# A two-layer vision kernel on one core: quotient of the recurrence by logarithm and Newton step, gated products of the second attention split, bias rows moved

## The chip, the cores and the metric

The kernel runs on one core of one Trainium2 chip. The metric is the device time of one execution in microseconds. The kernel before was run three times: median 424.29 us, lowest 422.48, highest 426.02.

## What is computed

64 images (3 x 64 x 64) become 1024 tokens of 192 channels; then come four blocks on these, each added to its input. The reference, cut to what matters here:

```
h = tok(x)                                   # shifted patches, layernorm, product with W
h = h + attention0(layernorm(h))             # 12 heads, 16 tokens per image
h = h + experts(layernorm(h))                # 8 experts, top 2, gates; y = gelu(x w1 + b1) w2 + b2
h = h + rwkv(layernorm(h))                   # below
h = h + attention1(layernorm(h))             # qkv has a gated low-rank part, below

# rwkv: forward and backward scans over the 16 tokens of an image, then
y  = (ef * af + eb * ab + ec * vt) / (ef * bf + eb * bb + ec)
x  = x + sigmoid(h @ Wr_a.T) * y @ Wo_a.T
x  = x + sigmoid(h @ Wr_f.T) * (square(relu(h @ Wk_f.T)) @ Wv_f.T)

# attention1
combine = top-2 gates of softmax(x @ Wg.T + bg)          # 8 experts
hw    = (x @ A + ba) * combine                           # rank 16 of each expert: 128 rows
qkv   = x @ Wqkv.T + bqkv + 2 * (hw @ Bm + combine @ bb)
out   = softmax(q k^T / 4) v @ Wproj.T + bproj
```

## The kernel before

The program is written out by hand for the five engines; each runs its own list in order and waits on semaphores. Tokens lie in eight tiles of 128; `hf` is a half of four tiles, `pr` a pair of tiles. The accumulator memory (PSUM) has eight banks, and `plan_fills` (a count over the whole program) gives each result a bank in turn; TensorE waits in `free` until the reader of the bank's last content has gone. To keep precision with f16 products, every operand is split into a high part (ScalarE rounds it to f16) and a low part (VectorE subtracts). So for nearly every step there is a chain: TensorE fills a bank, ScalarE copies the high part, VectorE subtracts the low part, TensorE multiplies both. `busy(name, n)` issues n products on TensorE (`early_a`, 128x512) that nobody reads.

*Experts.* Step u of 16 makes two chunks of 128 hidden units: TensorE multiplies (`h`), ScalarE applies Gelu twice (L871, L876), VectorE subtracts (L1406), and in the step after TensorE makes `y`, which VectorE adds to H with the gate (L1420). The rows `b2x`, `sel` and the clear of `ct3` (L1383 to L1391) are made by VectorE ahead of step 0, and ScalarE waits for them (`sel_ready`) before it copies the transposed gates behind step 3. In step 3 VectorE reads the logits of the second router (L1295), whose bank is one that the next chunks want.

*Recurrence.* 192 channels x 1024 tokens are three blocks of 128x512. `RECURRENCE_ORDER` sets the order of VectorE: `maxima`, `states` (four scans, L1473 and L1475), `sums` (two products, L1514 and L1515) and `outputs`. GpSimd makes one product per block for `states` (`weighted`) and three for the sums (`denominator`). TensorE adds three f32 terms each into `num` and `den`. `outputs` then is, on VectorE,

```
V.scalar_tensor_tensor(start(Af, b), start(rT, b), 1.0, bank(("num", b)), ALU.add, ALU.mult)   # L1521
V.reciprocal(start(E2b, b), bank(("den", b)))                                                  # L1526
V.tensor_tensor(start(E1b, b), start(Af, b), start(E2b, b), ALU.mult)                          # L1528
V.tensor_tensor(sy_lo[b], start(E1b, b), sy_hi[b], ALU.subtract)                               # L1530
```

with ScalarE's copy `sy_hi` (L931) between the last two. The output products `wo` follow, then a layernorm and the feed-forward part (`ffn_low`, `ffn_out`).

*Second attention.* VectorE does `ffn_out(1)`, clears `cstack` (L1582), does `x_low`, `gates_by_rank(0)` (router and ranks, copied to `crep1`, L1589) and `gated(0)`: TensorE transposes `crep1` (bank `ce`) and makes `la = x A`; ScalarE copies `ce` three times (L977 to L979); VectorE subtracts (L1596) and makes `hwF = (la + ba) * ce` (L1603); ScalarE rounds it (L982); VectorE subtracts (L1606). Then it makes the statistics and normalizations of tiles 4 to 7. TensorE's `qkv(hf)` fills five slots (QA, KA, VA, KVB, QB), in each five products of x and four of the gated part, the gated ones between the fourth and fifth of x; all wait for the low part of `hw`. ScalarE rounds each slot (L799), VectorE takes the low part (L1152) and `spread` writes K and V into masked copies for each head (L1162, eight heads in slots 1 and 2, four in slot 3). `ATTENTION_ORDER` is the same for both attentions: in it the second set of value transposes (`values1`) stands ahead of `qkv` of the second half. `gated(1)` stands ahead of `values1`. In VectorE's list it is called by `probabilities` between `softmax_in` (L1175 to L1178) and the second `values` (L1193).

## Time and profile before

| what | us |
|---|---|
| time of the profiled execution | 423.5 |
| its span, first to last instruction | 421.7 |
| TensorE busy | 373.2 (88%) |
| VectorE busy | 353.7 (84%) |
| ScalarE busy | 216.4 (51%) |
| GpSimd busy | 115.6 (27%) |
| mean granted clock of TensorE | 0.954 of full |
| median of three runs | 424.29 |

1.8 us of the execution lie around its span. Lines such as L1526 are lines of the kernel above. In the rows PE is TensorE, DVE VectorE, ACT ScalarE, POOL GpSimd. R, Q, T are large on-chip arrays that most tiles share, PS is PSUM, so that a row's place in time says more of it than its names. A duration in a row is from start to end of one instruction (or of the first to the last of `xN`); instructions of one engine overlap by some 0.1 us.

### The profile page before, as it was taken

To read this page: it belongs to the slowest core of one execution; us is meant where nothing else is said; L and a number is where in the kernel's file an instruction comes from. 1 tells how busy PE (TensorE), PEld (TensorE's weight loads), DVE (VectorE), ACT (ScalarE), POOL (GpSimd) and SP (SyncE) were. 2 spreads that over 40 slices of the span, in tenths; PEclk is the share of its full clock that TensorE was granted. 3 is DMA by queue.
4 is the path that set the end of the run, shared out by engine and by line. 5 is a ranking of instruction groups with operands and counts; after the bars stand their busy time and mean duration, and the time that the engine had idled before them with its cause. 6 is when DMAs were issued, how large, how long until landed. Compare 5 with 4: busy or idle time off the path is not lost.

```text
span 421.7 us, 8868 instructions
## 1 busy us (share of the span) xinstructions
PE 373.2 (88%) x3571; PEld 256.5 (61%) x3571; DVE 353.7 (84%) x787; ACT 216.4 (51%) x364; POOL 115.6 (27%) x151
## 2 busy tenths in 40 slices
PE   2999999797998999999779998887999787797997
PEld 2999958486665675676634443343597336645864
DVE  2979598998879799888989999988998689867872
ACT  2696286656656686796327662011871132454261
POOL 2745307212544481344231286103001010000000
PEclk9999998999598999999999999999999998699996
DMA  7856000400440000000000000000000000000101
GB/s 254 334 150 265 1 2 2 170 3 2 177 193 2 1 2 2 0 2 2 0 2 0 2 0 0 0 2 0 2 2 2 0 2 2 2 0 2 40 3 37
DMA packets 4233, 17.50 MB, mean 42 GB/s; under 512 B 857, under 2 KB 1762, under 8 KB 3682
## 3 DMA queue, kind: packets, MB, share of 16 engines
q1 hardware_dynamic: 4194, 16.95, 10.9%
q8 instruction: 28, 0.46, 0.4%
q14 instruction: 11, 0.09, 0.1%
HBM read 16.16 MB, written 0.79 MB: 40 GB/s over the span
## 4 chain that ended last, share of the span: by engine, by line
DVE 47%; PE 36%; issue 7%; ACT 5%; POOL 2%; DMA 1%; SPq 0%; DVEq 0%; POOLq 0%; ACTq 0%
PE PS L1631 31%; DVE R L1162 5%; DVE R L1475 3%; DVE R L1473 3%; DVE Q L1152 2%; PE PS L1783 2%; DVE H L1420 2%; DVE R L1048 2%; DVE R L1526 2%; POOL rstd L576 2%; DMA T<-tok_w 1%; DVE Q L1406 1%; ACT Q L956 1%; DVE Q L1178 1%; DVE smx L1177 1%
## 5 line engine op out<-in xcount | busy, mean ns | idle before, releaser
L573 POOL TENSOR_SCALAR ve<-mv 128x2 f32<-128x2 f32 (+1 forms) x36 | 10.5, 292 | 125.7 <-DVE mv L1068 102.9
L1631 PE MATMUL PS<-X_hi,R 128*128 128x512 f16 x144 | 39.9, 381 | 0.7 <-DVE gat L1295 0.4
L1631 PE MATMUL PS<-m,Q 128*128 128x192 f16 x384 | 35.4, 251 | 3.2 <-DVE Q L1406 1.9
L1631 PEld LDWEIGHTS PS<-m,Q 128*128 128x128 f16 x384 | 32.5, 100 | 7.1 <-issue 3.1
L1631 PE MATMUL PS<-Q,R 64*64 64x32 f16 (+11 forms) x1024 | 30.6, 193 | 6.9 <-DVE Q L1215 4.4
L1631 PEld LDWEIGHTS PS<-Q,R 64*64 64x64 f16 (+1 forms) x1024 | 29.5, 110 | 9.1 <-issue 6.0
L1631 PE MATMUL PS<-early_a 128*128 128x512 f16 x149 | 35.0, 386 | 0.0
L1631 PE MATMUL PS<-R,K 128*128 128x512 f32 x66 | 31.7, 598 | 3.4 <-DVE R L1515 3.4
L1162 DVE TENSOR_SCALAR R<-Q,K 128x1024 f16<-128x1024 f16 x80 | 32.6, 479 | 0.3
L1631 PE MATMUL PS<-X_hi,late_a 128*128 128x512 f16 (+1 forms) x72 | 26.1, 382 | 6.7 <-DVE X_hi L1142 4.2
L1420 DVE SCALAR_TENSOR_TENSOR H<-PS,gat,H 128x192 f32<-128x192 f32 x64 | 23.0, 410 | 7.2 <-PE PS L1631 6.9
L576 POOL TENSOR_TENSOR rstd<-ve,mhalf 128x2 f32<-128x2 f32 (+1 forms) x36 | 24.8, 690 | 3.0
L871 ACT ACTIVATE Q<-PS,col 128x512 f32<-128x512 f32 x32 | 22.2, 693 | 6.5 <-DVE Q L1406 6.3
L781 ACT ACTIVATE R<-PS 128x1024 f16<-128x1024 f16 x16 | 15.7, 1017 | 17.8 <-PE PS L1783 17.8
L1631 PEld LDWEIGHTS PS<-X_hi,R 128*128 128x128 f16 x144 | 14.2, 99 | 16.8 <-issue 0.8
L1631 PEld LDWEIGHTS PS<-early_a 128*128 128x128 f16 x149 | 14.2, 99 | 15.9 <-issue 0.7
L1631 PEld LDWEIGHTS PS<-R,K 128*128 128x128 f32 x66 | 12.2, 189 | 18.8 <-issue 12.7
L1406 DVE TENSOR_TENSOR Q<-Q 128x512 f16<-128x512 f32 x32 | 22.8, 750 | 0.4 <-ACT Q L876 0.2
L1783 PE MATMUL PS<-id,R 128*128 128x128 f16 x256 | 18.7, 240 | 4.6 <-DVE Q L1204 2.5
L876 ACT ACTIVATE Q<-PS,col 128x512 f16<-128x512 f32 x32 | 22.3, 697 | 0.0
L1631 PE MATMUL PS<-R 128*128 128x192 f32 x128 | 22.2, 328 | 0.1
L1631 PE MATMUL PS<-X_hi,late_b 128*128 128x512 f16 (+1 forms) x72 | 22.0, 379 | 0.0
(246 smaller groups left out, 928.9 us busy)
## 6 DMA issues: line engine op xcount, KB each, us to landing
R<-tok_x SPq DMA_DIRECT2D x8, 480.0 KB, 3.9
T<-tok_w SPq DMA_DIRECT2D x6, 480.0 KB, 7.1
R<-late SPq DMA_DIRECT2D x1, 2632.0 KB, 9.0
T<-moe SPq DMA_DIRECT2D x1, 2304.0 KB, 8.5
T<-moe SPq DMA_DIRECT2D x1, 1728.0 KB, 7.4
R<-full SPq DMA_DIRECT2D x1, 1152.0 KB, 12.3
R<-early SPq DMA_DIRECT2D x1, 776.0 KB, 10.3
out<-H SPq DMA_DIRECT2D x4, 192.0 KB, 1.9
```

What stands on the lines that cost most here:

```text
L573: nc.gpsimd.tensor_scalar(ve[:, t:t + w], mv[:, t:t + w, 1], EPS, None, ALU.add).then_inc(pool_step, 1)
L576: nc.gpsimd.tensor_tensor(rstd[:, t:t + w], ve[:, t:t + w], mhalf[:, 0:w], ALU.pow).then_inc(rstd_ready, 1)
L781: nc.scalar.activation(VA[:, hl, 8 * g:8 * g + 8, :], bank(name).bitcast(F16).rearrange("p (s n) -> p s n", s=8), ACT.Copy).then_inc(v_act ...
L871: nc.scalar.activation(ge[n % 3], bank(("h", n)), ACT.Gelu, bias=b, scale=1.0 / WS).then_inc(act_step, 1)
L876: nc.scalar.activation(hgh[slot], bank(("h", n)), ACT.Gelu, bias=b, scale=1.0 / WS).then_inc(gelu_ready, 1)
L1162: ins = V.tensor_scalar(v[:, :, :, h], w, K[:, mask + h:mask + h + 1], None, ALU.mult)
L1406: V.tensor_tensor(hgl[slot], ge[n % 3], hgh[slot], ALU.subtract).then_inc(hp_ready, 1)
L1420: ins = V.scalar_tensor_tensor(H[:, t], bank(name)[:, C * j:C * j + C], gat[:, 5, t, e:e + 1], H[:, t], ALU.mult, ALU.add)
L1473: link(V.tensor_tensor_scan(dst[:, 0:HALF][:, ::-1], d0, d1[:, ::-1], 0.0, op0, op1))
L1475: link(V.tensor_tensor_scan(dst[:, 1:BW], d0, d1, 0.0, op0, op1))
L1631: return T_.matmul(o, w, x, start=start, stop=stop, skip_group_check=True)
L1783: last = T_.transpose(o[:, P * s:P * s + P], VAbd[:, hl, 8 * g + s], id16[:])
```

## The change

Three parts.

1. *Bias rows.* The three clearings go to GpSimd, ahead of its clearing of `rW0`, and the five small operations become `bias_rows`, called in step 2 of the experts. The clearing of `cstack` goes to GpSimd too, behind the first `wo`.
2. *Quotient.* The product with `r` of block 0 and its Tanh come ahead, beside k and v of block 0 (nine unread products instead of 14). TensorE makes the sums in the order of `QUOTIENT_SUMS`. ScalarE takes Ln of `den` and Exp of the negative; VectorE refines with one Newton step and multiplies (`quotient`); `outputs` is gone. The low parts are steps of their own, the third one behind the first `wo_out`. `sums(1)` stands ahead of `states(2)`. The sign of the Tanh's argument is turned, and with it the sign of both factors.
3. *Gated products.* `adapted(hf)` makes the five products of x for the first two (second half: three) slots with no wait for the gates, then with a wait for the high half (`hw_high_ready`) their three products with it, then with a wait for the low half the rest. The second output pair of `ffn_out(1)` and the statistics of tiles 4 to 7 stand between `gates_by_rank(0)` and `gated(0)` on VectorE. In the second half `gated(1)` comes ahead of `qkv`, and `values1` comes behind `pt`. The unread products of `qkv` (8 and 13) are gone, eight of the 20 before the router too; eight come behind the second router.

```
+                    ("sums", 1), ("states", 2), ("sums", 2), ("quotient", 0), ("quotient", 1), ("low", 0), ("low", 1),
+                    ("quotient", 2))
+QUOTIENT_SUMS = (("num", 0), ("den", 0), ("num", 1), ("den", 1), ("den", 2), ("num", 2))
+SY_HIGH = {0: 1, 1: 2, 2: 5}
+SY_LOW = {0: 4, 2: 6}
+KVR_ORDER = (("k", 0), ("v", 0), ("r", 0), ("k", 1), ("k", 2), ("v", 1), ("v", 2), ("r", 1), ("r", 2))
...
             def decay_steps():
 
                 pool.wait_ge(psum_filled, f.done["pj", 0, 1, 1])
+                nc.gpsimd.memset(b2x[:], 0.0)
+                nc.gpsimd.memset(sel[:], 0.0)
+                nc.gpsimd.memset(ct3[:], 0.0).then_inc(rows_clear, 1)
                 nc.gpsimd.memset(rW0[:], 0.0).then_inc(pool_step, 1)
...
+            weighted(0)
+            weighted(1)
+            denominator(0)
+            weighted(2)
+            denominator(1)
+            denominator(2)
+            pool.wait_ge(psum_filled, f.done["wo", 0])
+            nc.gpsimd.memset(cstack[0:96, :], 0.0).then_inc(stack_clear, 1)
...
-                                   "r": (rT, ACT.Tanh, 0.5 / WS)}[n]
+                                   "r": (rT, ACT.Tanh, -0.5 / WS)}[n]
...
+            def logarithm(b):
+                filled(("den", b))
+                nc.scalar.activation(start(E2b, b), bank(("den", b)), ACT.Ln).then_inc(log_ready, 1)
+
+            def inverse(b):
+                y = start(E2b, b)
+                act.wait_ge(log_ready, b + 1)
+                nc.scalar.activation(y, y, ACT.Exp, scale=-1.0).then_inc(inverse_ready, 1)
+
             def sy_high(b):
-                act.wait_ge(sy_ready, 2 * b + 1)
+                act.wait_ge(sy_ready, SY_HIGH[b])
                 nc.scalar.activation(sy_hi[b], start(E1b, b), ACT.Copy).then_inc(hi_ready, 1)
                 hn[0] += 1
 
-            kvr(("k", 0), ("v", 0))
+            kvr(("k", 0), ("v", 0), ("r", 0))
             x_high_affine("mix1", (2, 3))
...
-            kvr(("r", 0), ("r", 1), ("r", 2))
-            for b in range(3):
-                sy_high(b)
+            kvr(("r", 1), ("r", 2))
+            for b in range(2):
+                logarithm(b)
+                inverse(b)
+            sy_high(0)
+            logarithm(2)
+            sy_high(1)
+            inverse(2)
+            sy_high(2)
...
+                hn[0] += 1
+
+            def hw_high(hf):
+                sl = slice(HALF * hf, HALF * (hf + 1))
                 act.wait_ge(hw_ready, 2 * hf + 1)
-                nc.scalar.activation(hw_hi[:, sl], hwF, ACT.Copy).then_inc(hi_ready, 1)
-                hn[0] += 2
+                nc.scalar.activation(hw_hi[:, sl], hwF, ACT.Copy).then_inc(hw_high_ready, 1)
             x_high("attn1", (0, 1))
             gate_exp(3, 0)
             gated(0)
+            hw_high(0)
             attention(1, {("st", 0): lambda: x_high("attn1", (2, 3)), ("values0", 0): lambda: gate_exp(4, 1),
-                          ("values1", 0): lambda: gated(1)})
...
                     scores_sum(0)
-                    probabilities(0, lambda: gated(1))
-                for i in range(5):
-                    low(1, i)
-                probabilities_low(0)
-                spread(1, 1)
+                    values(0, 0)
+                    softmax_in(0, 0)
+                    softmax_in(0, 1)
+                    gated(1)
+                    softmax_out(0)
+                    gated_low(1)
+                    softmax_out(1)
+                    for i in range(4):
+                        low(1, i)
+                    spread(1, 1, range(0, 4))
+                    low(1, 4)
+                    probabilities_low(0)
+                    values(0, 1)
+                    spread(1, 1, range(4, HA))
...
+            def bias_rows():
+
+                dve.wait_ge(rows_clear, 1)
+                for r in (0, 32):
+                    link(V.tensor_scalar(b2x[r:r + E], b2s[:], 4.0, None, ALU.mult))
+                    V.tensor_scalar(sel[r:r + E].rearrange("p a (k r) -> p (a k) r", r=32),
+                                    K[r:r + E, K_ID + r:K_ID + r + E][:, :, None].broadcast_to([E, E, 32]), 0.25, None,
+                                    ALU.mult)
+                V.scalar_tensor_tensor(b2x[64:64 + E], b2s[:], 4.0, b2x[0:E], ALU.mult,
...
+                if u == 2:
+                    bias_rows()
                 if u == 3:
...
                 V.tensor_tensor(n, n, start(Mf, b), ALU.mult)
                 V.tensor_tensor(v, v, start(rK, b), ALU.mult).then_inc(prod_ready, 1)
 
-            def outputs(b):
+            def quotient(b):
+
                 dve.wait_ge(kvr_ready, KVR_ORDER.index(("r", b)) + 1)
-                name = ("num", b)
-                filled(name)
-                V.scalar_tensor_tensor(start(Af, b), start(rT, b), 1.0, bank(name), ALU.add,
-                                       ALU.mult).then_inc(bank_free[f.bank[name]], 1)
-                released(name)
-                name = ("den", b)
-                filled(name)
-                V.reciprocal(start(E2b, b), bank(name)).then_inc(bank_free[f.bank[name]], 1)
-                released(name)
-                V.tensor_tensor(start(E1b, b), start(Af, b), start(E2b, b), ALU.mult).then_inc(sy_ready, 1)
+                n, d, inv, t = ("num", b), ("den", b), start(E2b, b), start(E2f, b)
+                filled(d)
+                dve.wait_ge(inverse_ready, b + 1)
+                V.tensor_tensor(t, bank(d), inv, ALU.mult).then_inc(bank_free[f.bank[d]], 1)
+                filled(n)
+                V.scalar_tensor_tensor(start(Af, b), start(rT, b), 1.0, bank(n), ALU.subtract,
+                                       ALU.mult).then_inc(bank_free[f.bank[n]], 1)
+                released(d)
+                released(n)
+                link(V.scalar_tensor_tensor(inv, t, 2.0, inv, ALU.subtract, ALU.mult))
+                V.tensor_tensor(start(E1b, b), start(Af, b), inv, ALU.mult).then_inc(sy_ready, 1)
+
+            def sy_low_part(b):
                 next_high()
                 V.tensor_tensor(sy_lo[b], start(E1b, b), sy_hi[b], ALU.subtract).then_inc(sy_ready, 1)
...
+                {"maxima": maxima, "states": states, "sums": sums, "quotient": quotient, "low": sy_low_part}[step](b)
 
             def wo_out(t):
                 if t % 2 == 0:
+                    if t == 2:
+                        sy_low_part(2)
                     name = ("wo", t // 2)
...
-            link(V.memset(cstack[0:96, :], 0.0))
+            ffn_out(1, (0,))
...
-                next_high()
+
+            def gated_low(hf):
+                sl = slice(HALF * hf, HALF * (hf + 1))
+                dve.wait_ge(hw_high_ready, hf + 1)
                 V.tensor_tensor(hw_lo[:, sl], hwF, hw_hi[:, sl], ALU.subtract).then_inc(hw_ready, 1)
 
             x_low("attn1", (0, 1))
             gates_by_rank(0)
+            ffn_out(1, (1,))
+            seen[4] = ln_stats_pair(4, H)
+            seen[6] = ln_stats_pair(6, H)
             gated(0)
+            def last_norms(t):
+                for i in (t, t + 1):
+                    ln_norm(i, H, seen[t], xc[0])
+                    xc[0] += 1
+            last_norms(4)
+            gated_low(0)
+            last_norms(6)
             attention(1, lambda pr: dve.sem_inc(h_ready, 1))
...
+                def adapted(hf):
+
+                    first = 3 if hf else 2
+                    xa, xb = X_hi[:, 4 * hf:4 * hf + 4, 0], X_hi[:, 4 * hf:4 * hf + 4, 1]
+                    xl = X_lo[:, 4 * hf:4 * hf + 4]
+                    sl = slice(HALF * hf, HALF * (hf + 1))
...
+                    for i in range(first):
+                        base(i)
+                    pe.wait_ge(hw_high_ready, hf + 1)
+                    for i in range(first):
+                        with_high(i)
+                    pe.wait_ge(hw_ready, 2 * hf + 2)
+                    for i, (s, o, m) in enumerate(SLOTS):
+                        if i >= first:
+                            base(i)
+                            with_high(i)
+                        mm(bank(("qkv", a, hf, s))[0:m], fullp[:, 0, FW + o:FW + o + m], hw_lo[:, sl], False,
+                           True).then_inc(psum_filled, 1)
+
                 def qkv(hf):
-                    c0 = 0 if a == 0 else LATE["qkv1"]
+                    if a == 1:
+                        return adapted(hf)
                     if x_pairs:
...
                     if (a, step, hf) == (1, "pj", 1):
                         busy((step, a, hf), 4)
-                    if a == 1 and step == "qkv":
-                        busy((step, a, hf), 13 if hf else 8)
...
-                added(("den", b), (ident, start(Bf, b)), (ident, start(Bb, b, 1)), (ident, start(rK, b)))
+            kvr(("r", 1), ("r", 2))
+            for which, b in QUOTIENT_SUMS:
+                if which == "num":
+                    pe.wait_ge(prod_ready, b + 1)
+                    pe.wait_ge(num_ready, b + 1)
+                    added(("num", b), (ident, start(Af, b)), (ident, start(rV, b)), (ident, start(Ab, b, 1)))
+                else:
+                    pe.wait_ge(ew_ready, 3 * b + 3)
+                    pe.wait_ge(den_ready, b + 1)
+                    added(("den", b), (ident, start(Bf, b)), (ident, start(Bb, b, 1)), (ident, start(rK, b)))
...
+
+            def second_router():
+                gate_router(1)
+                busy("values", 8)
+
+            attention(1, None, {("st", 0): lambda: turn("attn1", (2, 3)), ("values0", 0): second_router,
+                                ("qkv", 1): lambda: gated(1)})
```

ScalarE in the recurrence, from the last Exp of the decays to the copies of the quotient: before (L919 decay, L927 state weights, L904 Tanh of r, L931 copy of the quotient),

```order
L919 ACTIVATE R<-R 128x512
L927 ACTIVATE R<-PS 128x512 x2
L927 ACTIVATE R<-PS,col 128x512
L904 ACTIVATE R<-PS 128x512 x3
L931 ACTIVATE Q<-R 128x512 x3
```

and now behind the Tanh, up to the copy of the second quotient (L947 Ln, L952 Exp, L956 copy):

```order
L947 ACT_TABLE_LOAD
L947 ACTIVATE R<-PS 128x512
L952 ACT_TABLE_LOAD
L952 ACTIVATE R<-R 128x512
L947 ACT_TABLE_LOAD
L947 ACTIVATE R<-PS 128x512
L952 ACT_TABLE_LOAD
L952 ACTIVATE R<-R 128x512
L956 ACTIVATE Q<-R 128x512
L947 ACT_TABLE_LOAD
L947 ACTIVATE R<-PS 128x512
L956 ACTIVATE Q<-R 128x512
```

A table load stands ahead of each Ln and each Exp, five here and the sixth behind the last row.

VectorE in the recurrence, before, from the end of `states(2)` (L1505) through `sums(1)` and the first two `outputs`,

```order
L1473 SCALAR_TENSOR_TENSOR R<-R,Q 128x512
L1505 MEMSET R 128x33 x4
L1514 TENSOR_TENSOR R<-R 128x512
L1515 TENSOR_TENSOR R<-R 128x512
L1521 SCALAR_TENSOR_TENSOR R<-R,PS 128x512
L1526 RECIPROCAL R<-PS 128x512
L1528 TENSOR_TENSOR R<-R 128x512
L1530 TENSOR_TENSOR Q<-R,Q 128x512
L1514 TENSOR_TENSOR R<-R 128x512
L1515 TENSOR_TENSOR R<-R 128x512
L1521 SCALAR_TENSOR_TENSOR R<-R,PS 128x512
L1526 RECIPROCAL R<-PS 128x512
```

and now, from the end of `states(2)` (L1560) through `sums(2)`, the first two quotients and their low parts:

```order
L1560 MEMSET R 128x33 x4
L1569 TENSOR_TENSOR R<-R 128x512
L1570 TENSOR_TENSOR R<-R 128x512
L1578 TENSOR_TENSOR R<-PS,R 128x512
L1580 SCALAR_TENSOR_TENSOR R<-R,PS 128x512
L1584 SCALAR_TENSOR_TENSOR R<-R 128x512
L1585 TENSOR_TENSOR R<-R 128x512
L1578 TENSOR_TENSOR R<-PS,R 128x512
L1580 SCALAR_TENSOR_TENSOR R<-R,PS 128x512
L1584 SCALAR_TENSOR_TENSOR R<-R 128x512
L1585 TENSOR_TENSOR R<-R 128x512
L1589 TENSOR_TENSOR Q<-R,Q 128x512 x2
```

The reciprocals are gone, `sums(2)` stands ahead of every quotient, and the two low parts stand behind both.

TensorE at the second half of the second attention, before, from the value transposes (L1783, L1791) to the first slot (`R,fullp` are gated products),

```order
L1783 MATMUL PS<-id,R 128x128 x32
L1791 MATMUL PS<-id,R 64x64 x32
L1631 MATMUL PS<-early_a 128x512 x13
L1631 MATMUL PS<-X_hi,late_a 128x512
L1631 MATMUL PS<-X_lo,late_a 128x512
L1631 MATMUL PS<-X_hi,late_a 128x512
L1631 MATMUL PS<-X_hi,late_b 128x512
L1631 MATMUL PS<-R,fullp 128x512 x4
L1631 MATMUL PS<-X_hi,late_b 128x512
```

and now the products of x of the second and third slot, and the gated ones of the first three:

```order
L1704 MATMUL PS<-X_hi,late_a 128x512
L1704 MATMUL PS<-X_lo,late_a 128x512
L1704 MATMUL PS<-X_hi,late_a 128x512
L1704 MATMUL PS<-X_hi,late_b 128x512 x2
L1704 MATMUL PS<-X_hi,late_a 128x512
L1704 MATMUL PS<-X_lo,late_a 128x512
L1704 MATMUL PS<-X_hi,late_a 128x512
L1704 MATMUL PS<-X_hi,late_b 128x512 x2
L1704 MATMUL PS<-R,fullp 128x512 x12
```

The gated products of the first slots stand behind the products of x of three slots, with no unread product ahead.

## Rows read from the trace of the kernel before

**Rows 1.** The page: part 1, granted clock of part 2 in 40 slices, part 4 by engine

```profile
PE 373.2 (88%) x3571; PEld 256.5 (61%) x3571; DVE 353.7 (84%) x787; ACT 216.4 (51%) x364; POOL 115.6 (27%) x151
...
PEclk9999998999598999999999999999999998699996
...
DVE 47%; PE 36%; issue 7%; ACT 5%; POOL 2%; DMA 1%; SPq 0%; DVEq 0%; POOLq 0%; ACTq 0%
```
**Rows 2.** Timeline of VectorE at the experts: start us, us, engine, line, tiles, idle before

```profile
122.90 1.70 DVE L1077 TENSOR_SCALAR xn<-H,mv,rstd 128x192 f32<-128x192 f32 x2 [0.34 <-POOL rstd L576]
...
124.97 0.14 DVE L1383 MEMSET T<- 96x96 uint32 x1
...
125.82 0.25 DVE L1387 TENSOR_SCALAR T<-b2s 8x192 f16<-8x192 f32 x1
...
128.06 1.29 DVE L1406 TENSOR_TENSOR Q<-Q 128x512 f16<-128x512 f32 x2
...
140.99 0.74 DVE L1420 SCALAR_TENSOR_TENSOR H<-PS,gat,H 128x192 f32<-128x192 f32 x2 [0.36 <-PE PS L1631]
```
**Rows 3.** Timeline of GpSimd and TensorE at the experts

```profile
122.82 1.38 POOL L633 MEMSET R<- 128x1539 f32 x1
...
119.41 0.38 PE L1631 MATMUL PS<-X_hi,R 128*128 128x512 f16 x1 [0.23 <-DVE H L1233]
...
129.41 3.37 PE L1631 MATMUL PS<-m,Q 128*128 128x192 f16 x24 [1.94 <-DVE Q L1406]
...
142.87 0.39 PE L1631 MATMUL PS<-X_hi,R 128*128 128x512 f16 x1 [0.35 <-DVE gat L1295]
```
**Rows 4.** Timeline of VectorE in the recurrence

```profile
262.85 0.68 DVE L1521 SCALAR_TENSOR_TENSOR R<-R,PS 128x512 f32<-128x512 f32 x1
...
263.56 3.36 DVE L1526 RECIPROCAL R<-PS 128x512 f32<-128x512 f32 x1
...
268.34 0.69 DVE L1530 TENSOR_TENSOR Q<-R,Q 128x512 f16<-128x512 f32 x1 [0.69 <-ACT Q L931]
...
282.37 0.55 DVE L1541 SCALAR_TENSOR_TENSOR T<-PS,T 128x384 f32<-128x384 f32 x1
```
**Rows 5.** Timeline of ScalarE: two table loads and an Exp

```profile
120.22 1.28 ACT L871 ACT_TABLE_LOAD   x1
...
226.12 1.28 ACT L917 ACT_TABLE_LOAD   x1
...
227.41 0.63 ACT L917 ACTIVATE R<-R 128x512 f32<-128x512 f32 x1
```
**Rows 6.** Timeline of TensorE in the recurrence

```profile
256.17 5.31 PE L1631 MATMUL PS<-R,K 128*128 128x512 f32 x12
```
**Rows 7.** Timeline of VectorE in the second attention

```profile
325.61 0.48 DVE L1582 MEMSET R<- 96x512 uint32 x1 [0.17 <-DVE H L1575]
...
336.53 0.75 DVE L1603 SCALAR_TENSOR_TENSOR R<-PS,col,R 128x512 f32<-128x512 f32 x1
...
338.59 0.35 DVE L1065 BATCH_NORM_STATS2 stats<-H 128x6 f32<-128x192 f32 x1
...
340.63 0.67 DVE L1077 TENSOR_SCALAR xn<-H,mv,rstd 128x192 f32<-128x192 f32 x2 [0.36 <-POOL rstd L576]
...
344.34 3.26 DVE L1162 TENSOR_SCALAR R<-Q,K 128x1024 f16<-128x1024 f16 x8
```
**Rows 8.** Waits of VectorE: us in total, times, longest us

```profile
DVE R L1596 <- ACT R L979: 4.6, 2, 2.5
...
DVE R L1606 <- ACT R L982: 1.4, 2, 0.7
```
**Rows 9.** Timeline of TensorE, one slot's gated products

```profile
339.60 1.03 PE L1631 MATMUL PS<-R,fullp 128*128 128x512 f16 x4
```
**Rows 10.** Groups of VectorE from 350 to 392: busy us, mean ns, idle before

```profile
L1152 DVE SCALAR_TENSOR_TENSOR Q<-PS,col,Q 128x512 f16<-128x512 f32 (+1 forms) x6 | 4.5, 746 | 3.9 <-ACT Q L799 3.9
```

120 lines of the change are left out of this document (59 added, 61 removed).

## The prediction

> **What bounds the kernel now.** I read the page first, then the timelines of VectorE, ScalarE and TensorE side by side around the three places of the diff, then the waits. The page says that this is a two-engine program: TensorE is busy 88% and VectorE 84% of a 421.7 us span, and the chain that ended last runs 47% on VectorE and 36% on TensorE, with ScalarE at 5% [rows 1]. So an instruction taken off VectorE shortens the run where VectorE never waits, and a wait is worth what the next engine does not take back. All times below are on the clock of the profiled execution: its span is 421.7, its own time 423.5, 0.8 under the median of the three runs (424.29), inside their spread.
>
> **Part A, bias rows of the experts.** Three clearings (124.97 to 125.82, 0.85 us) and five small operations (125.82 to 128.06, 2.24 us) stand on VectorE ahead of the first subtraction of the experts at 128.06 [rows 2]. TensorE waits for that subtraction: the first product of step 1 starts at 129.41 after 1.94 us idle [rows 3]. After the change the clearings are GpSimd's and the five come in step 2, ahead of the reading of the router's logits. TensorE's next products wait for that reading (start 142.87, released by L1295) [rows 3], so the five are paid again before the same point; the start gains 3.09 and hands back 2.24. What is left is 0.85, and 0.36 more because VectorE's wait at 140.99 [rows 2] is filled by the inserted work (a shorter one follows it): 1.4 at the most, say. Against that, GpSimd's clearings now number four in a row. The one that is there (L633, 122.82, 1.38 us) coincides with a pair of normalizations on VectorE that took 1.70 us [rows 2, 3]; such a pair will be seen to take 0.67 in part C1, so 1.0 was lost. The new ones are about as much memory again; if VectorE is held once more the gain falls to about 0.4, if twice to -0.6. I take 0.8, range -0.6 to 1.4. The three moved clearings cost GpSimd itself nothing: the decay rows behind them are not wanted before the recurrence. ScalarE's copies of the transposed gates now wait for the rows (end of step 2), which is about where TensorE delivers the transposes anyway.
>
> **Part B, the quotient.** Before, each of the three blocks does on VectorE: numerator (0.68), reciprocal (3.36), product (0.69), a wait of 0.69 for ScalarE's f16 copy, low part (0.69); the stretch from 262.85 to 282.37 is 19.5 us, with the two products of `sums(2)` inside [rows 4]. After, ScalarE does Ln and Exp(-x), and VectorE four operations of 0.7, about 2.8 a block with their links. VectorE alone would need 1.4 + 3 x 2.8 + 2 x 0.6 = 11.0. But ScalarE must swap its tables six times. The order shows the six loads; the trace shows one load (1.28) with an Exp of 0.63 starting 0.01 behind it [rows 5]. It also shows a load that ran at 120.22, at once after the instruction before it, though its Gelu's product, five matmuls 0.22 apart from 119.41 on, ended only near 120.6 [rows 3, 5]: a load does not wait for what its activation waits for, so a first load hides in idle time. Ln is in no row; I take 0.65, from the Exp on the same shape, with 0.6 and 1.3 (twice) as bounds, which move three steps of the chain by -0.1 or +1.9 in all and lie in the bounds below.
> The chain then, in steps. TensorE has `r0` behind it, so its sums start 5 x 0.22 earlier: 256.17 - 1.1 = 255.1, each numerator with denominator takes 5.3 [rows 6]: den0 is ready at 260.4, den1 at 265.6. ScalarE: Ln0 to 261.1, load, Exp to 263.0; load to 264.3; Ln1 265.6 to 266.3; load, Exp to 268.2; copy of block 0 to 268.7; load 270.0, Ln2 270.7; copy of block 1 (which waits for its quotient) at 271.7; load, Exp to 273.6. VectorE: `sums(2)` now ahead of all quotients, done 262.85 + 1.4 = 264.2; quotient 0 to 267.0; quotient 1 from 268.2 (1.2 waited) to 271.0; two low parts to 272.3, quotient 2 from 273.6 to 276.4. The next step there, `wo_out(0)`, started at 282.37: 6.0 earlier, less 0.6 for the third low part that now comes behind it. I take 5.4. Bounds: 3.5 if Ln takes double, or if GpSimd's products hit the rearranged ones of VectorE twice more, each time with the 1.0 lost in part A; 7.5 if VectorE alone bounds (19.5 - 11.0 = 8.5, less 0.6, rounded).
> The Trainium skill (ScalarE: Activation LUTs, "What ACT_TABLE_LOAD costs") puts a switch at 1283 ns for the load plus about 1380 ns of drain. The row agrees with the load and shows no drain behind it; by that page of the Trainium skill each of the five exposed loads would add 1.38, and the quotient part would gain next to nothing (rival 2).
>
> **Part C1, second attention, first half.** VectorE's gated product `hwF` starts at 336.53 and the first spread at 344.34, 7.81 later; in between are a wait of 0.70 for the high half, eight statistics (1.7), four normalizations, a wait of 0.36 for GpSimd and a second like it, then TensorE's first slot with all nine terms [rows 7, 8]. A pair of normalizations there takes 0.67. After: statistics stand ahead of `hwF`, in the 2.5 us in which VectorE waits for ScalarE's copies [rows 8], with one output pair of the feed-forward. What `hwF` gains: the clearing 0.48 and the wait 2.5 go, plus small gaps 0.5; 1.7 of statistics comes: 1.8. From `hwF` on: product 0.75, ScalarE's high copy 0.65, six gated products on two slots at 0.22 (1.03 for four, pipelined [rows 9]) 1.3, the low product and its tail 0.4, ScalarE's eviction 0.7, two low parts 1.4: 5.2 against 7.8. Ten ungated products (2.2) are done while the gated product is made, in the place of eight fillers. C1 = 1.8 + 2.6 = 4.4; bounds 3.0 (the statistics' pair collide with GpSimd) and 5.0.
>
> **Part C2, second half.** VectorE's waits there before: 2.1 for the copies of the gates, 0.7 for the high half, 3.9 for ScalarE's evictions of the five slots: 6.7 [rows 8, 10], and it waited about 0.5 for the score transposes, which ran at half clock: 7.2. After, the copies come ahead of the exponentials, the second half of softmax stands between `gated` and `gated_low`, and three slots are ungated before the high half is due. New waits: 0.4 for the last gate step, 0.4 for the first slot, and one that is new in kind. The second set of value transposes now comes behind the slots; ScalarE copies three banks of about 1.0 before the output products may begin, and VectorE, done with two spreads, waits for the outputs twice, 1.2 and 1.1. Sum 3.1: gain 4.1. I take 3.9, a little for the clock; bounds 0.5 (next part) and 5.0.
>
> **Sum.** 0.8 + 5.4 + 4.4 + 3.9 = 14.5. 423.5 - 14.5 = 409.0; a median of new runs may lie 0.8 higher like that of the old, I put 409.4. A measurement of this kernel tells about 1% (4.2 us) from no change.
>
> **Rivals.**
> 1. TensorE's clock falls in the second attention. The page grants 0.8 and 0.6 of full speed in the two slices from 348 to 369, so half of it (1.2 GHz) for some ten us in all, after sparse work and idling [rows 1]. After the change TensorE has eight fillers there, but then idles some 3.4 us until the score sums; 13 and 8 fillers of the slots are gone. If it is at 1.2 GHz when the 15 ungated products of the second half run, these take 3.2 more, and the gated ones part of that: C2 falls from 3.9 to about 0.5: 412.8. Against it: before, the same place had gone through a longer idling and the next slice is at 0.9 again, before the slots run. Chance 0.20.
> 2. Table switches cost more than the one row of a load says, since the engine has to run empty first. If each exposed switch takes twice the 1.28 of its row, the chain above gives Exp0 at 264.3, Exp1 at 270.7, Exp2 at 278.2 and `wo_out(0)` at 281.0: B falls from 5.4 to 0.8, 414.0. The Trainium skill's section named above states such a drain. For it: six switches in 13 us are not in the trace. Against it: the 0.01 gap of rows 5. Chance 0.08.
> 3. Parts A and C2 are bounded by contention and by ScalarE's value copies harder than I read: A -0.6, C2 2.0: 412.7. Chance 0.12.
> 4. Slower than before. One mechanism: without the fillers (21 at the slots, 8 before the router) the clock falls at the idling before the first gated product and stays at 1.2 GHz through both halves. The slots are 90 products; each costs 0.22 more, 19.8 together, and this outweighs the gain of 14.5 from the 66th product on: 409.4 + 19.8 = 429.2. Against it: the slices around 336 stayed at 0.9 although there is idling there now, and no slice of 10.5 us but one shows 0.5 [rows 1]. Chance 0.02.
> 5. It does not do what it says: the sums of the six PSUM banks or `sums(2)` are late, and VectorE waits for denominators rather than dividing: B 2.5, 412.3. Chance 0.06.
> My forecast keeps 0.52. The likeliest's own range is 406.5 to 411.5; the range for 8 in 10 goes up to hold rivals 1, 3 and 5 and part of 2: 405.0 to 414.5. All but rival 4 are more than 1% below 424.29: faster 0.96, same 0.02, slower 0.02.
>
> **What would show it.** A: no wait of TensorE ahead of step 1; TensorE's products behind the router's reading near 142 instead of 142.87. B: six loads of 1.28 with activations directly behind them; no reciprocal of 128x512; `wo_out(0)` 6 to 7 us earlier, TensorE idle only near 273. C: VectorE's waits for copies of the gates gone; first spread 4.4 earlier relative to the feed-forward's end; value copies of ScalarE as the releaser of the output products. Wrong would be: loads with a gap behind them, a clock of 0.5 while the slots run, or VectorE's four quotient operations far from 0.7 each.

## The result and the profile after

The changed kernel takes 408.41 us (median of 4 runs, 407.01 to 409.70), the kernel before beside it 423.38 (4 runs, 422.45 to 426.02): ratio 0.9636, 95% interval 0.9576 to 0.9696. The profiled execution took 407.69, its span is 405.8, 15.9 less than before. Of all executions below one, 413.31 of e6, ran in a slower state and is left out of its median.

The page of the changed kernel, busy time, granted clock and chain (beside [rows 1]):

```profile
PE 365.1 (90%) x3544; PEld 251.6 (62%) x3544; DVE 347.8 (86%) x786; ACT 227.0 (56%) x376; POOL 118.7 (29%) x155
...
PEclk9999999989689999999999999999999999799996
...
DVE 50%; PE 32%; issue 7%; ACT 6%; POOL 2%; DMA 2%; SPq 1%; DVEq 0%; ACTq 0%; POOLq 0%
```

VectorE lost 5.9 us of work, TensorE 8.1, and ScalarE gained 10.6. Both large engines are busy for a larger share of the span (90% and 86%, before 88% and 84%): VectorE's idle time fell by 10.0, from 68.0 to 58.0, so most of the gain is waits that closed.

**Where the 15.9 us came from.** I cut both traces at seven instructions of VectorE that both kernels have and compare the distances between them: first router's logits read, second router's logits read, first output of `wo`, first square of the feed-forward, first and second gated product `hwF`, last addition to H.

| stretch | before | after | gain |
|---|---|---|---|
| start to first logits | 119.30 | 117.86 | 1.44 |
| to second logits (A) | 23.34 | 22.73 | 0.61 |
| to first `wo` output (B) | 139.73 | 133.90 | 5.83 |
| to feed-forward (B) | 16.43 | 17.25 | -0.82 |
| to first `hwF` (C1) | 37.73 | 36.27 | 1.46 |
| to second `hwF` (C1, C2) | 34.17 | 29.09 | 5.08 |
| to last addition (C2) | 48.11 | 45.81 | 2.30 |

The first line holds no changed instruction: what was changed gave 14.46. Of the 5.08, 2.38 lie between the first `hwF` and the first spread (C1), 2.70 behind it.

*Experts.* The timeline of VectorE (beside [rows 2], columns as there):

```profile
121.46 3.03 DVE L1113 TENSOR_SCALAR xn<-H,mv,rstd 128x192 f32<-128x192 f32 x2 [0.34 <-POOL rstd L586]
...
127.80 1.65 DVE L1459 TENSOR_TENSOR Q<-Q 128x512 f16<-128x512 f32 x2
...
136.55 0.24 DVE L1438 TENSOR_SCALAR T<-b2s 8x192 f16<-8x192 f32 x1
136.82 0.28 DVE L1439 TENSOR_SCALAR T<-K 8x256 f16<-8x256 f32 x1
...
137.70 0.35 DVE L1442 SCALAR_TENSOR_TENSOR T<-b2s,T 8x192 f16<-8x192 f32 x1
...
140.59 0.18 DVE L1345 TENSOR_SCALAR gat<-PS 128x32 f32<-128x32 f32 x1
```

The timeline of GpSimd, two of the four clearings and two decay steps:

```profile
121.82 0.94 POOL L645 MEMSET Q<- 96x1024 f16 x1
122.71 1.37 POOL L646 MEMSET R<- 128x1539 f32 x1
...
124.88 2.59 POOL L652 TENSOR_SCALAR R<-R,col 128x512 f32<-128x512 f32 x1 [0.79 <-DVE ndec L1431]
...
127.63 1.58 POOL L652 TENSOR_SCALAR R<-R,col 128x512 f32<-128x512 f32 x1
```

The timeline of TensorE (both beside [rows 3]):

```profile
127.19 2.14 PE L1704 MATMUL PS<-m,Q 128*128 128x192 f16 x24
...
140.83 0.39 PE L1704 MATMUL PS<-X_hi,R 128*128 128x512 f16 x1 [1.54 <-DVE gat L1345]
```

VectorE of the kernel before, one of the five small operations and the second pair of subtractions:

```profile
126.10 0.60 DVE L1388 TENSOR_SCALAR T<-K 8x256 f16<-8x256 f32 x1
...
131.06 1.29 DVE L1406 TENSOR_TENSOR Q<-Q 128x512 f16<-128x512 f32 x2
```

The pair of normalizations beside GpSimd's clearings takes 3.03 us instead of 1.70. The five small operations (136.55 to 138.05) stand ahead of the reading at 140.59, for which TensorE idles 1.54; at this place they take 1.50, where they had taken 2.24. The pair of subtractions at 127.80 takes 1.65 instead of 1.29. TensorE's first `y`, 24 products, takes 2.14 with no idle time ahead of it; before they took 3.37, with the clock low.

*Recurrence.* The timeline of VectorE from the first quotient to the first output of `wo` (beside [rows 4]; L1578 begins a quotient):

```profile
263.97 1.60 DVE L1584 SCALAR_TENSOR_TENSOR R<-R 128x512 f32<-128x512 f32 x1
...
266.22 0.69 DVE L1578 TENSOR_TENSOR R<-PS,R 128x512 f32<-128x512 f32 x1
...
271.77 0.69 DVE L1578 TENSOR_TENSOR R<-PS,R 128x512 f32<-128x512 f32 x1 [1.35 <-ACT R L952]
...
274.49 0.55 DVE L1602 SCALAR_TENSOR_TENSOR T<-PS,T 128x384 f32<-128x384 f32 x1
```

The timeline of ScalarE (beside [rows 5]; L947 Ln, L952 Exp):

```profile
253.86 1.28 ACT L947 ACT_TABLE_LOAD   x1
258.40 0.60 ACT L947 ACTIVATE R<-PS 128x512 f32<-128x512 f32 x1 [3.25 <-PE PS L1704]
259.01 1.28 ACT L952 ACT_TABLE_LOAD   x1
260.31 0.63 ACT L952 ACTIVATE R<-R 128x512 f32<-128x512 f32 x1
...
263.55 0.60 ACT L947 ACTIVATE R<-PS 128x512 f32<-128x512 f32 x1 [1.31 <-PE PS L1704]
```

The first load runs at 253.86, 4.5 us ahead of its Ln: it hides. The load ahead of the second Ln (260.95 to 262.23) hides too, since that Ln waits 1.31 longer for TensorE. The other four are 1.28 long, each with its activation 0.01 to 0.02 behind it. Ln takes 0.60. VectorE divides the first two blocks with no wait (266.22 carries none) and waits once, 1.35, for the third Exp. One Newton operation took 1.60 instead of 0.69, beside a product of GpSimd.

*Second attention.* The timeline of VectorE (beside [rows 7, 8]; the last two are the low parts of the outputs):

```profile
328.01 0.75 DVE L1662 SCALAR_TENSOR_TENSOR R<-PS,col,R 128x512 f32<-128x512 f32 x1
...
331.99 1.41 DVE L1188 SCALAR_TENSOR_TENSOR Q<-PS,col,Q 128x512 f16<-128x512 f32 x2 [1.26 <-ACT Q L815]
...
373.27 0.42 DVE L1261 TENSOR_TENSOR Q<-PS,Q 128x256 f16<-128x256 f32 x1 [0.95 <-ACT Q L838]
...
375.22 0.42 DVE L1261 TENSOR_TENSOR Q<-PS,Q 128x256 f16<-128x256 f32 x1 [1.09 <-ACT Q L838]
```

The timeline of TensorE there (beside [rows 9]):

```profile
344.64 3.57 PE L1704 MATMUL PS<-early_a 128*128 128x512 f16 x8
...
358.56 2.78 PE L1704 MATMUL PS<-R,fullp 128*128 128x512 f16 x12 [1.11 <-ACT R L1018]
...
370.00 7.86 PE L1704 MATMUL PS<-Q,R 128*128 128x96 f16 x256 [1.43 <-ACT R L802]
```

The eight unread products at 344.64 ran at half clock (0.45 us each against 0.22), but the twelve gated ones at 358.56 at full clock. The output products at 370.00 wait for ScalarE's value copies, as forecast, and VectorE for the outputs twice.

### The profile page after: what moved, and what is told of

It reads as the page before. It is cut to its first block, busy times and chain, and to the rows that moved or that the text cites. A ratio compares the mean times of both kernels' runs of the same rounds, so it can differ in the third digit from the quotient of the medians.

```text
span 405.8 us, 8821 instructions
## 1 busy us (share of the span) xinstructions
PE 365.1 (90%) x3544; PEld 251.6 (62%) x3544; DVE 347.8 (86%) x786; ACT 227.0 (56%) x376; POOL 118.7 (29%) x155
## 4 chain that ended last, share of the span: by engine, by line
DVE 50%; PE 32%; issue 7%; ACT 6%; POOL 2%; DMA 2%; SPq 1%; DVEq 0%; ACTq 0%; POOLq 0%
PE PS L1704 28%; DVE R L1198 4%; DVE R L1528 3%; DVE R L1530 3%; DVE H L1473 3%; DVE Q L1188 2%; DVE Q L1459 2%; DVE R L1084 2%; DMA T<-tok_w 2%; DVE R L1230 1%; POOL rstd L586 1%; ACT Q L987 1%; DVE R L1570 1%; DVE Q L1215 1%; DVE smx L1214 1%
## 5 line engine op out<-in xcount | busy, mean ns | idle before, releaser
L1704 PE MATMUL PS<-m,Q 128*128 128x192 f16 x384 | 34.2, 246 | 1.2 <-DVE R L1494 0.6
L1704 PEld LDWEIGHTS PS<-m,Q 128*128 128x128 f16 x384 | 31.6, 98 | 4.8 <-issue 3.1
L1704 PE MATMUL PS<-early_a 128*128 128x512 f16 x122 | 30.7, 404 | 0.0
L1704 PEld LDWEIGHTS PS<-R 128*128 128x128 f32 x128 | 20.6, 190 | 0.5 <-ACT R L752 0.3
L1704 PE MATMUL PS<-X_hi,late_b 128*128 128x512 f16 (+1 forms) x72 | 20.4, 379 | 0.0
L1704 PEld LDWEIGHTS PS<-early_a 128*128 128x128 f16 x122 | 11.9, 101 | 13.6 <-issue 2.4
```

The costliest lines, as they stand in the source:

```text
L1704: return T_.matmul(o, w, x, start=start, stop=stop, skip_group_check=True)
```

## The experiments

Twelve kernels. All have the same stretches, so each gets a row of distances, in us (start | A | to `wo` | to feed-forward | to `hwF` | `hwF` to spread | to second `hwF` | to the end):

| run | start | A | wo | ff | hwF | spread | hwF 2 | end |
|---|---|---|---|---|---|---|---|---|
| before | 119.30 | 23.34 | 139.73 | 16.43 | 37.73 | 7.81 | 34.17 | 48.11 |
| after | 117.86 | 22.73 | 133.90 | 17.25 | 36.27 | 5.43 | 29.09 | 45.81 |
| e1 | 120.36 | 22.73 | 140.27 | 16.43 | 37.73 | 7.81 | 34.17 | 48.42 |
| e2 | 120.16 | 22.89 | 133.89 | 17.24 | 37.72 | 7.81 | 34.18 | 45.54 |
| e3 | 120.58 | 22.89 | 140.26 | 16.43 | 36.24 | 5.43 | 29.08 | 45.44 |
| e4 | 121.41 | 21.39 | 134.55 | 17.25 | 36.25 | 5.43 | 29.07 | 42.89 |
| e5 | 121.31 | 22.73 | 136.89 | 19.79 | 36.25 | 5.42 | 29.08 | 45.52 |
| e6 | 119.67 | 22.73 | 132.53 | 17.77 | 36.25 | 5.43 | 29.08 | 42.89 |
| e7 | 119.29 | 22.73 | 133.90 | 17.25 | 36.25 | 5.43 | 29.67 | 45.75 |
| e8 | 120.37 | 20.36 | 133.88 | 17.25 | 36.26 | 5.42 | 29.08 | 45.60 |
| e9 | 119.61 | 22.74 | 134.39 | 17.23 | 36.24 | 5.42 | 29.07 | 42.89 |
| e10 | 119.34 | 20.36 | 133.87 | 17.24 | 36.24 | 5.43 | 29.07 | 42.88 |
| e11 | 119.81 | 20.19 | 133.87 | 17.24 | 36.24 | 5.42 | 29.07 | 42.89 |
| e12 | 117.61 | 22.73 | 133.90 | 17.24 | 36.26 | 5.43 | 29.07 | 42.89 |

Where two kernels have the same code in a stretch and the clock is full, the distance repeats within 0.03 us. A low stretch of the clock lies inside 134.55 of e4 (granted 0.50 from 143.5 to 146.8 and from 218.6 to 221.9), 134.39 of e9 (217.6 to 220.9) and 19.79 of e5. Effects of tenths are read here, not in the medians, whose runs spread by 1.5 to 5 us and come from several chips (e9, e10 and e11 share one).

**e1, part A alone**

The first of the three parts of the change, without the clearing of `cstack`:

```
+                nc.gpsimd.memset(ct3[:], 0.0).then_inc(rows_clear, 1)
...
+                if u == 2:
+                    bias_rows()
```

> The kernel before with part A alone (GpSimd clears the rows, the five bias-row operations in step 2 of the experts). Theory: the parts act in different stretches and add up, so this one gives its 0.6 us of the changed kernel: the second router's logits are read 0.6 us earlier, counted from the read of the first router's logits (before: 142.64 - 119.30 = 23.34; here 22.7), and the time is 423 within the spread. The pair of normalizations beside GpSimd's four clearings takes about 3.0 us (1.70 before). Rival: the 0.6 was an accident of clock levels around 130 us and the pair's loss outweighs the gain: 23.3 or more, 424.

Measured: 423.02 (10 runs), before 423.89 (13 runs), ratio 0.997, interval 0.9939 to 1.0002. The distance is 22.73, as in the changed kernel. Runs e2 and e3, which lack part A, show 22.89, not 23.34: there the clock stayed full where it had fallen in the kernel before (its 24 products of `y` took 2.15 in e2 and 3.37 in [rows 3], after the same idle time of 1.94). So 0.16 of the 0.61 is work, 0.45 is a low stretch that happened to be in one profile. TensorE of e2, the 24 products:

```profile
130.26 2.15 PE L1660 MATMUL PS<-m,Q 128*128 128x192 f16 x24 [1.94 <-DVE Q L1429]
```

**e2, part B alone**

The second part, with GpSimd's new order:

```
+QUOTIENT_SUMS = (("num", 0), ("den", 0), ("num", 1), ("den", 1), ("den", 2), ("num", 2))
...
+            def quotient(b):
```

> The kernel before with part B alone (sums before quotients, Ln and Exp on ScalarE, one Newton step). Theory: its 5.0 us stand alone, the feed-forward part begins 5.0 earlier than before and all behind it moves by the same: 418.4. A third of a wait may differ, since r of block 0 comes ahead: range 417.5 to 419.5. Rival: part of B's gain in the changed kernel came from the second attention's start being better placed (clock), so alone it gives less: 420 or more; or the second attention, unchanged, gives something back by its filler products.

Measured: 417.39 (416.39 to 418.26), before 423.89, ratio 0.985, 0.9791 to 0.9908; this is just under the range that was expected. From second logits to feed-forward 151.13 against 156.16: 5.03 alone, 5.01 in the changed kernel, so B does not lean on the other parts. The profile gains 2.57 more in the last stretch, whose code is that of before: no low clock there.

**e3, part C alone**

The third part, with the clearing of `cstack` on GpSimd:

```
+                def adapted(hf):
...
+            def gated_low(hf):
```

> The kernel before with part C alone (statistics moved ahead, slots with the high half first, value transposes behind, fillers moved). Theory: 3.8 us from the first half and 5.4 from the second, 9.2 in all, and 0.35 given back at the tail: 414.6, range 413.5 to 416. Rival: the second half's gain (1.5 more than I forecast) rests on where the clock's low stretch falls, which here is elsewhere in time, so it is 3.9 or less: 416 or more.

Measured: 414.51 (412.86 to 416.81), before 423.89, ratio 0.9779, 0.9716 to 0.9841. The three stretches of C give 1.49, 5.09 and 2.67: 9.25, against the 9.2 of the theory.

**e4, the three clearings behind the decay steps**

```
-                nc.gpsimd.memset(b2x[:], 0.0)
-                nc.gpsimd.memset(sel[:], 0.0)
-                nc.gpsimd.memset(ct3[:], 0.0).then_inc(rows_clear, 1)
                 nc.gpsimd.memset(rW0[:], 0.0).then_inc(pool_step, 1)
...
                 ins.then_inc(w0_ready, 1)
+                nc.gpsimd.memset(b2x[:], 0.0)
+                nc.gpsimd.memset(sel[:], 0.0)
+                nc.gpsimd.memset(ct3[:], 0.0).then_inc(rows_clear, 1)
```

> The changed kernel with GpSimd's three new clearings moved behind the four decay steps of the same routine (GpSimd idles there from 131 to 141 us; the rows are wanted at 136.5). Theory (contention): the second pair of normalizations falls from 3.03 us to the 1.70 that it took in the kernel before beside one clearing, TensorE's transposes behind it (1.25 idle) come 1.3 earlier, and the read of the second router's logits comes 1.0 to 1.3 earlier than 140.59 - 117.86 = 22.73 after the first: about 21.6. In total about 407.3. Rival: the pair's time was not on the path (TensorE had other work behind, VectorE the five operations), so the read moves by less than 0.3 and nothing is gained.

VectorE of e4, the same pair and the same reading:

```profile
125.01 1.70 DVE L1113 TENSOR_SCALAR xn<-H,mv,rstd 128x192 f32<-128x192 f32 x2 [0.34 <-POOL rstd L586]
...
142.80 0.18 DVE L1345 TENSOR_SCALAR gat<-PS 128x32 f32<-128x32 f32 x1
```

The pair is back at 1.70 and the distance falls by 1.34, just the 1.33 of the pair: the collision was on the path. Median 406.97 (404.22 to 409.08).

**e5, two more table loads**

```
             sy_high(1)
+            nc.scalar.activation(spare[:, 0:1], ones[:, 0:1], ACT.Exp)
+            nc.scalar.activation(spare[:, 1:2], ones[:, 0:1], ACT.Ln)
             inverse(2)
```

> The changed kernel with a one-column Exp and a one-column Ln put between the second copy of the quotient and the last Exp on ScalarE, so that two more table loads stand there, where VectorE already waits 1.35 us for that Exp. Theory (a switch costs its load and no more): two loads of 1.28 and two small activations of some 0.2, 3.0 in all, each activation 0.01 behind its load; VectorE's wait ahead of the third quotient grows from 1.35 to 4.3, and the first output of the recurrence, counted from the second sums, comes 3.0 later. Time 411.4. Rival (the engine also drains at a switch, 2.66 a switch as in the Trainium skill, ScalarE: Activation LUTs): 5.7 later, 414.1. Other rival: hidden by TensorE's idle time and given back: under 1 later.

The timeline of ScalarE in e5, the two added switches:

```profile
273.14 1.28 ACT L977 ACT_TABLE_LOAD   x1
274.44 0.20 ACT L977 ACTIVATE spare<-ones 128x1 f32<-128x1 f16 x1
274.64 1.28 ACT L978 ACT_TABLE_LOAD   x1
275.94 0.20 ACT L978 ACTIVATE spare<-ones 128x1 f32<-128x1 f16 x1
```

VectorE of e5, the third quotient, which waited 1.35 in the changed kernel:

```profile
278.20 0.69 DVE L1581 TENSOR_TENSOR R<-PS,R 128x512 f32<-128x512 f32 x1 [4.35 <-ACT R L953]
```

The distance to the first `wo` output is 136.89 against 133.90: 2.99 later, as the theory without a drain has it. A switch costs its load of 1.28 and nothing beyond. The Trainium skill (ScalarE: Activation LUTs, "What ACT_TABLE_LOAD costs") adds about 1.38 of drain to each; the run disagrees, since two of them would have made it 5.7. In this profile the clock then fell, and the stretch behind took 19.79 instead of 17.25. Median 412.41 (411.56 to 416.58), 4.0 over 408.41, of which the stretches give 3.0.

**e6, without the Newton step** (it leaves out the refinement of the reciprocal)

```
-                V.tensor_tensor(t, bank(d), inv, ALU.mult).then_inc(bank_free[f.bank[d]], 1)
+                dve.sem_inc(bank_free[f.bank[d]], 1)
...
-                link(V.scalar_tensor_tensor(inv, t, 2.0, inv, ALU.subtract, ALU.mult))
```

> The changed kernel without the Newton step (it leaves out the refinement of the reciprocal; the sign of the Tanh's argument and of the sum with it goes back): two of VectorE's four operations of each quotient go. Theory: in quotients 0 and 1 VectorE is the bound, 2 x 2 x 0.66 = 2.6 plus the 0.9 of the one that collides with GpSimd, but quotient 1 then waits for ScalarE's Exp (265.46 + 0.63 in the changed kernel), and of quotient 2, behind Exp 2, 1.3 more goes; Exp 2 waits for quotient 1's copy, so the first output comes 1.3 to 2.5 earlier, I take 1.9: 406.5. Rival: ScalarE's six loads are the bound throughout and the Newton step is free: under 0.5.

VectorE of e6, the quotients of the second and third block and the first output:

```profile
268.13 0.69 DVE L1580 SCALAR_TENSOR_TENSOR R<-R,PS 128x512 f32<-128x512 f32 x1 [1.97 <-ACT R L952]
...
273.53 0.69 DVE L1580 SCALAR_TENSOR_TENSOR R<-R,PS 128x512 f32<-128x512 f32 x1 [1.46 <-ACT R L952]
...
274.93 0.55 DVE L1601 SCALAR_TENSOR_TENSOR T<-PS,T 128x384 f32<-128x384 f32 x1
```

1.37 earlier at `wo`, at the low end of my 1.3 to 2.5, of which 0.52 is given back behind it: 0.85 in all, under my 1.9 and over the 0.5 of the rival. Of six operations removed only the two of the last block count; the first four become waits for Exp. Median 408.49 (three runs, 405.60 to 410.30), which says nothing of an effect of this size.

**e7, without the eight products behind the second router**

```
-                busy("values", 8)
+                busy("values", 0)
```

> The changed kernel without the eight unread products behind the second router (TensorE idles 3.6 us more there). Theory of my rival 1: these are what lets the clock rise again before the slots of the second half; without them the 15 ungated products and part of the 12 gated ones run at 1.2 GHz and the second half ends 1.5 to 3.4 us later: 410 to 412. Rival: TensorE ran these eight at half clock (3.57 us) in time that it would have idled, and the clock rises as before with the 64 value transposes behind them: no change, 408.4, or a few tenths earlier since the transposes start earlier.

TensorE of e7, value transposes and score transposes:

```profile
353.03 1.06 PE L1897 MATMUL PS<-id,R 64*64 64x64 f16 x32
354.02 1.54 PE L1907 MATMUL PS<-K,Q 128*128 128x128 f32 x6
```

Neither number held. The clock rose some 3 to 4 us later than with these products, the score transposes took 1.54 instead of 0.87, VectorE waited 0.50 for them, and the second `hwF` came 0.58 later; but the clock was full again before the slots, and nothing more was lost. Median 409.95 (407.47 to 410.57).

**e8, the five operations on GpSimd as well**

```
+                for r in (0, 32):
+                    nc.gpsimd.tensor_scalar(b2x[r:r + E], b2s[:], 4.0, None, ALU.mult).then_inc(pool_step, 1)
+                    nc.gpsimd.tensor_scalar(sel[r:r + E].rearrange("p a (k r) -> p (a k) r", r=32),
...
+                nc.gpsimd.tensor_scalar(rows4[:], b2s[:], 4.0, None, ALU.mult).then_inc(pool_step, 1)
...
+                nc.gpsimd.tensor_tensor(b2x[64:64 + E], rows4[:], b2x[0:E], ALU.subtract).then_inc(pool_step, 1)
...
-                if u == 2:
-                    bias_rows()
```

> The kernel of the run before last on part A (three clearings behind the decay steps) with the five bias-row operations on GpSimd behind them too, none on VectorE. Theory: these five are on the path to the reading of the second router's logits (1.53 us, and TensorE idles 1.53 ahead of its products behind that reading), so the distance between the two readings of logits falls from 21.39 to 19.9, and TensorE's wait there to 0.1; the time falls by 1.5 from 406.97: 405.5. Rival: GpSimd's small operations hit VectorE's subtractions and additions (f32, SBUF) and lengthen them, or GpSimd is late with the rows and ScalarE's copy of the transposed gates holds the Gelus: distance 21 or more.

VectorE of e8, the subtractions of steps 2 and 3 beside GpSimd's small operations:

```profile
135.22 1.43 DVE L1476 TENSOR_TENSOR Q<-Q 128x512 f16<-128x512 f32 x2
...
137.87 1.63 DVE L1476 TENSOR_TENSOR Q<-Q 128x512 f16<-128x512 f32 x2
```

Distance 20.36: 1.03 less than e4, not 1.5. 0.5 went to the subtractions (1.28 undisturbed). Median 407.16 (405.81 to 407.53).

**e9, the changed kernel once more**, with no edit

> The changed kernel itself once more, on another run. Both theories on the noise: if the spread of times comes from where the clock's low stretches fall and from the start, then the distances between milestones repeat to 0.05 us where the clock is full (second logits to feed-forward 151.15, feed-forward to first gated product 36.25, that to the second 29.09), and only the start (first logits 117.9 before, 119.3 to 121.4 in the others) and the last stretch (43.9 without a low stretch, 46.4 to 46.8 with one) differ. Time 407 to 410. Rival: the stages themselves vary by some tenths.

407.05 (406.24 to 409.19), ratio 0.9623, 0.9579 to 0.9667. The distances of A, C1 and the first part of C2 repeat to 0.03; 0.5 more stands ahead of `wo`, where the clock was low from 217.6 to 220.9, and the last stretch is 42.89 instead of 45.81. The two profiles of one kernel differ by that and by the start (119.61 against 117.86).

**e10 and e11, four unread products in the last gap; GpSimd's order turned round**

```
+                        if (a, hf, pr) == (1, 1, 1):
+                            busy("tail", 4)
...
                 pool.wait_ge(psum_filled, f.done["pj", 0, 1, 1])
+                pool.wait_ge(decay_ready, 1)
                 nc.gpsimd.memset(b2x[:], 0.0)
```

e10 is e8 with the first edit; e11 is e10 with the second, and the clearing of `rW0` and the decay steps put behind the rows.

> The kernel with the bias rows on GpSimd, and four more unread products of TensorE in the 0.93 us that it idles between the two pairs of probability transposes of the last attention half. Theory: this idle time is what lets the clock fall to half a few us later (in 7 of 10 profiles), which costs 2.6 us in the last output products; filled, the last stretch takes 43.9 in the profile and the median falls from 407.2 to about 405.3. Rival: the fall does not hang on this gap (other gaps in the 12 us before, or the sparse products of 32 columns behind it): the last stretch takes 46.4 to 46.8 as often as before and the median stays at 407.

> The same kernel, and GpSimd does nothing until VectorE's pair of normalizations is done: then the bias rows, and the clearing of the decay rows with the decay steps last. Theory (contention is with one-source operations of VectorE on f32): the second pair of normalizations takes 0.67 instead of 1.70, the clearings now run beside subtractions of two sources, which hold their 0.64 each, and the distance between the two readings of logits falls from 20.36 to 19.4; 1.0 less in all. Rival: the clearings and small operations lengthen the subtractions and gate operations instead, or ScalarE gets the rows late: 20.4 or more.

The timeline of VectorE in e11:

```profile
123.40 0.67 DVE L1133 TENSOR_SCALAR xn<-H,mv,rstd 128x192 f32<-128x192 f32 x2 [0.34 <-POOL rstd L589]
...
130.29 0.56 DVE L1391 TENSOR_TENSOR Q<-gat 128x256 f32<-128x256 f32 x1
...
132.72 0.58 DVE L1444 TENSOR_SCALAR gat<-gat 128x32 f32<-128x32 f32 x1
...
139.34 0.74 DVE L1493 SCALAR_TENSOR_TENSOR H<-PS,gat,H 128x192 f32<-128x192 f32 x2 [0.25 <-PE PS L1722]
```

TensorE of e10, the four products in what was the gap:

```profile
389.81 1.03 PE L1721 MATMUL PS<-early_a 128*128 128x512 f16 x4
390.80 0.55 PE L1936 MATMUL PS<-K,Q 128*128 128x128 f32 x3
```

e10: **403.27 us** (6 runs, 402.74 to 404.25), before beside it 422.77, ratio 0.9527, 0.9494 to 0.9560, against 407.05 of the changed kernel on the same chip: the lowest median here, and under the 405.3 expected. e11: 404.09 (402.59 to 406.32), ratio 0.9549. In e11 the pair took its 0.67 as expected, but the distance fell by 0.17 only: small gate operations beside GpSimd took 0.56 and 0.58 (0.42 and 0.18 in the changed kernel), and VectorE waits for ScalarE (0.46) ahead of them and for TensorE (0.25) behind them. The collision of the pair is gone, and other collisions and waits took its place.

**e12, the changed kernel with the first of these two edits alone**

> The changed kernel with nothing else than the four unread products between the last two probability transposes. In the profiles so far the last stretch (from the second gated product on) took 46.4 to 49.4 us with a low clock in 7 of 11 kernels without these products and had none in the 2 with them. Theory: the gap of 0.93 us is what the fall hangs on: the last stretch is 43.9 in the profile and the six times lie within 2 us of each other, with a median 1.5 to 2.4 below 407.05 and 408.41, near 405.5. Rival: it was the GpSimd rows or chance: median 407 to 408, spread 3 us, the last stretch again 46.4 or more in the profile.

407.31 (7 runs, 404.47 to 408.22), ratio 0.9601, 0.9569 to 0.9633. The profiled run was the fastest, its last stretch 42.89 with a mean clock of 0.977; five of the other six had 0.966 and 407.2 to 408.2. So the median is the rival's. The gap alone does not bring the fall either: e4, e6 and e9 have it and kept the clock in the last stretch. Whether filling it keeps the clock up is not shown, since the five runs at 0.966 have no trace, and e9 had 0.966 with its last stretch at full clock. What stays open is why four of e10's six runs had 0.974 or more and e12's, on another chip, mostly 0.966. Of e10's 3.8 in the medians 2.4 are the A stretch; between the two profiles (3.2) 0.5 more is e9's low stretch ahead of `wo` and 0.3 the start. The other 1.4 of the medians I can't place.

## Why the prediction was right, and where it was off

The forecast was 409.4, range 405.0 to 414.5; 408.41 and 407.05 were measured. The sum of the change, 14.5, was met by 14.46, and that it came so close is partly luck: A, B and C1 fell short by 0.2, 0.4 and 0.6, C2 went over by 1.1, and 0.45 of A is a low stretch of the clock in the profile of before.

- **A, 0.8 forecast, 0.61 in the pair of profiles, 0.16 as work.** The step "if VectorE is held once more the gain falls to about 0.4" was the right one to take: the pair went from 1.70 to 3.03, and e4 shows that this 1.33 is on the path. Three more terms were off or missing. The five operations hand back 1.5, not 2.24, since those that took 0.60 and 0.66 beside GpSimd's decay step take 0.28 at the new place. The second pair of subtractions lost 0.37 and a gate operation 0.10 beside GpSimd, which I had not reckoned. And of the waits that would be filled, the one at 140.99 came with the low clock (e2 does not have it), while 0.35 was filled at full clock as well. Against e2 this gives 3.1 - 1.5 - 1.33 - 0.47 + 0.35, which is the 0.16 within 0.01.
- **B, 5.4 forecast, 5.01.** The first output came 5.83 earlier (forecast 6.0), 0.82 is given back behind it (0.6 forecast for the third low part). The forecast's times are on the clock of the profile of before, where the second logits stand 2.05 later (142.64 against 140.59); moved by that, the chain came as forecast: second quotient at 268.27 (268.2), end of the third Exp at 273.68 (273.6), first output at 276.54 (276.4). VectorE's wait of 1.2 ahead of the second quotient did not show, because VectorE was late by as much: GpSimd's product held the first quotient by 0.9, and `sums(2)` ended some 0.4 late beside GpSimd (its second product took 1.59). The wait for the third Exp did come (1.35). e6 confirms that the third block's chain through Exp is the bound, e5 that a switch is worth its load: rival 2 is out, by a run made for it.
- **C1, 4.4 forecast, 3.84.** 1.46 ahead of `hwF` (1.8), 2.38 behind it (2.6): two sizes, no step.
- **C2, 3.9 forecast, 5.00** (2.70 and 2.30; 5.36 up to where the clock falls in the last stretch, whose low part then costs the changed kernel 0.36 more than the kernel before). The new waits were forecast at 3.1 and are 2.8 (0.50, 0.25, 0.95, 1.09). The step that was mis-sized is what goes, 7.2 in the forecast. From the first copies of the values to the next set VectorE's idle time fell from 8.2 (35.77 less 27.56 busy) to 3.5 (30.77 less 27.28), by 4.7; the windows follow below. In it is a wait that I had left out, ahead of the residual addition (0.38, now 0.15). Busy time fell by 0.3 as well, which I had at nothing; 0.2 of it is that evictions that follow one another overlap (three took 2.07, three apart 3 x 0.75). The last 0.3 to 0.4 lies behind that window: VectorE waits 0.53 instead of 0.85 for the next score transposes.
- **Rival 1** (clock at half while the slots of the second half run): did not happen, nor without the eight products (e7). They are worth 0.6. **Rival 3**: contention was harder than read, the value copies were not. **Rival 4**: the clock was full through the slots of both halves; the twelve gated products at 358.56 took 2.78. **Rival 5**: the sums were in time, no quotient of VectorE waited for TensorE.
- The 1.44 of the start belongs to no part: the first 118 us, with the same code, took 117.6 to 121.4 in fourteen profiles. The prediction had allowed 0.8 between a profile and the median; the start alone varies by 3.8.

The windows for C2, of the kernel before (us, then busy of PE, PEld, DVE, ACT, POOL with counts, granted clock, DMA share, GB/s):

```profile
362.68:398.45 35.77, 32.65 (x480) 22.94 (x479) 27.56 (x58) 14.28 (x22) 0.00 (x0) 0.96 0.01 3
```

and of the changed kernel, the same 58 instructions of VectorE:

```profile
351.78:382.55 30.77, 28.23 (x449) 20.30 (x444) 27.28 (x58) 13.89 (x23) 0.00 (x0) 1.00 0.01 2
```

The last stretch shows what the clock does. A window of the changed kernel 40 us behind the second `hwF`:

```profile
397.10:401.10 4.00, 4.00 (x21) 2.34 (x19) 1.22 (x3) 0.00 (x0) 0.00 (x0) 0.50 0.00 0
```

and the same of e4, whose code is the same there, and which is through with its products at the end of it:

```profile
399.92:403.92 4.00, 2.85 (x27) 1.87 (x25) 1.62 (x4) 0.00 (x0) 0.00 (x0) 1.00 0.14 49
```

At 0.50 the output products take about 0.19 us each (21 in 4.00) instead of 0.11 (27 in 2.85), and the stretch takes 45.81 instead of 42.89. The clock fell there in 7 of 11 profiles without the four products and in none of 3 with them; by e12 this does not show that they prevent it. Up to where the clock falls, 38 us behind the second `hwF`, every instruction of VectorE and ScalarE in the changed kernel stands within 0.1 us of where it stands in e4 and e9, which kept the clock, so nothing in the order or the time of the work tells such runs apart.

## What to carry to other kernels

Cut both traces at instructions that both kernels have and compare distances: these repeat to a few hundredths where medians differ by a per cent, and what differs in a stretch of unchanged code (start, clock) shows itself as such. A function replaced by two table-driven ones can be priced as the sum of its loads plus activations along the chain, with loads that stand ahead of a wait free. Work moved to an idle engine should be placed where it does not lengthen its neighbour's instructions: here the same three clearings cost 1.3 us at one place and nothing 8 us later.

## What I had not expected of the hardware

- GpSimd's MEMSET, which reads nothing, held VectorE's one-source f32 normalizations for as long as it ran (pair 0.67, 1.70, 3.03 with no, one, and four clearings beside it: e11, e4, changed kernel). Two-source subtractions kept their 1.28 beside the same clearings (e11). Beside GpSimd's decay steps one of the two lost, in the changed kernel the one that began second: subtractions from 124.81 kept 1.29, and the decay step from 124.88 took 2.59 instead of 1.58; the next decay step, from 127.63, kept 1.58, and the subtractions from 127.80 took 1.65 instead of 1.29. Beside GpSimd's arithmetic on 8 partitions they took 1.43 to 1.63 (e8), and in the recurrence a product took 1.60 instead of 0.69.
- After the same 1.94 us of idle time the clock fell in one profile (24 products in 3.37) and not in another (2.15, e2).
- A GpSimd operation on 8 partitions by 192 took 0.68 to 1.04 us (e8, e11), where VectorE took 0.24 to 0.35.
